# Vision tower block on one core: first embedding issued before the constants, first feed-forward group prepared inside the attention pass, third group's first score tile ahead of the value products

## The reference, cut to what matters

```python
h = _L0_tok_ref(x, W, b)                                   # patches @ W.T + b
h = concatenate([cls_tok, h], axis=1)                      # (128, 197, 256)
h = h + attn(layernorm(h))    # 16 heads of 16; q and k pass through low-rank maps and an RMS norm,
                              # causal softmax, output map per head
h = h + ffn(layernorm(h))     # 3 cycles of: coupling = 0.1 + ar*(0.7*gf + 0.3*tf - 0.5)*2
                              #              out = out + coupling * twist(out)
# tf: four-layer net per token (256-256-128-64-1); gf: three-layer net on the token mean, once
```

## Time and profile before

| what | value |
|---|---|
| median of 3 runs | 3697.5 us (3697.17 to 3704.69) |
| the profiled execution | 3697.29 us |
| its span in the trace | 3694.3 us |
| PE busy | 3538.2 us (96% of the span) |
| DVE busy | 3062.1 us (83%) |
| ACT busy | 2420.7 us (66%) |
| POOL busy | 1808.5 us (49%) |
| mean granted TensorE clock | 0.991 of full speed |

### The profile page before, as it was taken

The page is one execution under the profiler, slowest core; times in us unless marked ns, Lnnn a source line. Parts: engine busy times, 40 slices in busy tenths (PEclk is TensorE's granted clock), DMA queues, the critical chain, the costliest instruction groups (busy, mean ns, idle before and its releaser), DMA issues.

```text
span 3694.3 us, 86493 instructions
## 1 busy us (share of the span) xinstructions
PE 3538.2 (96%) x30479; PEld 2654.2 (72%) x30734; DVE 3062.1 (83%) x7295; ACT 2420.7 (66%) x5698; POOL 1808.5 (49%) x2960
## 2 busy tenths in 40 slices
PE   6999999999999999999999999996999999999998
PEld 5888888888888888888888888874555555555554
DVE  6888888888888888888888888875989989989987
ACT  3777777777777777777777777773554554554553
POOL 3666766667666776667766776663001101101000
PEclk9999999999999999999999999997999999999999
DMA  3444444444444444444444444433212222222211
GB/s 99 111 112 114 116 115 112 115 111 119 113 110 115 115 119 110 113 111 119 119 104 113 117 119 104 116 88 92 69 56 79 74 59 78 73 61 78 73 44 53
DMA packets 298315, 361.65 MB, mean 98 GB/s; under 512 B 28193, under 2 KB 264993, under 8 KB 297889
## 3 DMA queue, kind: packets, MB, share of 16 engines
q1 hardware_dynamic: 297888, 356.11, 36.7%
HBM read 131.80 MB, written 53.26 MB: 50 GB/s over the span
## 4 chain that ended last, share of the span: by engine, by line
PE 77%; DVE 9%; DMA 8%; issue 3%; SPq 1%; POOL 1%; ACT 1%; another core or an unknown queue 0%; DVEq 0%; POOLq 0%; ACTq 0%
PE ps L1357 12%; PE ps L1052 11%; PE ps L1100 7%; PE ps L1087 6%; PE ps L1366 6%; PE ps L1170 5%; PE ps L1124 5%; PE ps L1139 5%; PE ps L1189 4%; DMA mx_scratch<-mxT 4%; PE ps L1179 3%; DMA qZ<-mx_scratch 3%; PE ps L1381 2%; PE ps L1373 2%; PE ps L1147 2%
## 5 line engine op out<-in xcount | busy, mean ns | idle before, releaser
L1052 PE MATMUL ps<-xb,w_tok 128*128 128x196 f32 x3072 | 684.7, 347 | 0.3 <-DVE small L766 0.3
L862 DVE TENSOR_REDUCE mx<-ps 69x2 f32<-69x396 f32 x1024 | 520.8, 557 | 147.2 <-PE ps L1179 147.2
L1357 PE MATMUL ps<-X,cn_w 128*128 128x394 f32 x1536 | 584.5, 510 | 0.4 <-issue 0.4
L558 ACT ACTIVATE p<-ps 128x394 f32<-128x394 f32 x1024 | 454.5, 499 | 122.1 <-PE ps L1100 112.0
L1052 PEld LDWEIGHTS ps<-xb,w_tok 128*128 128x128 f32 x3072 | 490.3, 191 | 0.4 <-issue 0.4
L856 DVE TENSOR_REDUCE mx<-ps 128x4 f32<-128x512 f32 x512 | 339.0, 683 | 168.7 <-remote 168.0
L538 POOL TENSOR_SCALAR ve<-mv 128x4 f32<-128x4 f32 x64 | 19.8, 310 | 920.5 <-DVE mv L921 920.5
L1357 PEld LDWEIGHTS ps<-X,cn_w 128*128 128x128 f32 x1536 | 273.9, 190 | 250.5 <-issue 94.9
L1100 PE MATMUL ps<-qZ,kT 128*128 128x396 f32 (+1 forms) x2048 | 379.4, 319 | 48.2 <-DMA qZ<-mx_scratch 46.6
L509 POOL TENSOR_TENSOR h<-h,att 128x256 f32<-128x256 f32 (+1 forms) x256 | 187.3, 752 | 410.7 <-DVE att L851 410.7
L470 POOL TENSOR_SCALAR_AFFINE_SELECT p<-p 128x512 f32<-128x512 f32 x512 | 338.0, 660 | 78.0 <-ACT p L558 60.5
(11 more groups left out here) (140 smaller groups left out, 7932.2 us busy)
## 6 DMA issues: line engine op xcount, KB each, us to landing
qZ<-qT SPq DMA_DIRECT2D x256, 396.0 KB, 5.2
xb<-in_x SPq DMA_DIRECT2D x128, 588.0 KB, 7.2
kZ<-kT SPq DMA_DIRECT2D x512, 128.0 KB, 2.7
h_scratch<-h SPq DMA_DIRECT2D x128, 128.0 KB
hl<-h_scratch SPq DMA_DIRECT2D x64, 256.0 KB
hk<-h_scratch SPq DMA_DIRECT2D x64, 256.0 KB
out<-hk SPq DMA_DIRECT2D x64, 256.0 KB
h_scratch<-h SPq DMA_DIRECT2D x128, 69.0 KB
```

What stands on the lines that cost most here:

```text
L558: s.activation(p0[:, i, 2 * jj:2 * jj + 2, :], ps[:, (b0, b1)[jj], 0:2 * TE].rearrange("p (a b) -> p a b", b=TE)[:, :, 0:T], ACT.Exp).then ...
L862: v.tensor_reduce(mx[:T1, 1, 4 * i + c:4 * i + 4:2], ps[:T1, SBANK[3 * i + 1 + c], 0:2 * TE].rearrange("p (a b) -> p a b", b=TE), AX.X, AL ...
L1052: mm = t_.matmul(ps[:, W[ft], 0:NP], w_tok[:, k, ft * P:ft * P + P], xb[:, par, k, :], start=k == 0, stop=k == KT - 1)
L1357: mm = t_.matmul(ps[:, 2 * c + mt, 0:N2], cn_w1[:, f, mt * P:mt * P + P], X[:, c, state(cyc), f, :], start=f == 0, stop=f == FT - 1)
```

## The change

1. **Preamble.** The loads are split: `w_tok`, `tok_bT` and `clsT` on a semaphore `s_e` with the first image between them; nine small ones (`s_w`); the second image; 17 later ones (`s_w2`). The order on SP's queue is `w_tok`, image 0, `tok_bT`, `clsT`, the nine, image 1, the 17. PE embeds image 0 after `s_e`, the image and the two cleared banks; the weight products move behind this embedding into step -3. The clearing of `qkv`, `k2`, `q2`, `qZ` and `kZ` moves from DVE to POOL, behind its masks; SP's and ACT's steps wait for it. DVE's seven constants for the second pass move behind its last step.
2. **Between the passes.** `hl` of quad 0 is loaded by SP in step 126 (`n == B - 2`). DVE's `stats2` for its four pieces and `apply2` for two are put in step 129, `apply2` for the other two in step 130; POOL's `norm2` for pieces 0 and 1 stands in step 129 ahead of the masking of the exponents (`select`), for 2 and 3 behind it. `hl`, `hn2`, `st2`, `ve2`, `rstd2` move to addresses behind those of the first pass. PE waits for the last value division (`att_ready`) and then transposes quad 0. The three layers of `gnet` for quad 0 go between the layers of the first phase, in banks `GB0`.
3. **Each step.** `scores_first(m, 2)`, with its wait for the second half of `kZ`, moves ahead of both `pv`. Banks 0 and 1 change places in `SBANK` from the third group on, in `KB`, `QB`, `MB` and `CB`; the first tile of the third group so waits for two maxima instead of four.
4. **End.** For pieces 2 and 3 of the last quad, both `bases` come before both `update`.

```diff
-        SBANK = (6, 7, 0, 1, 2, 3, 0, 1, 2, 3, 0, 5)
-        MAX_OF = (4, 2, 5, 6, 7)
+        SBANK = (6, 7, 0, 1, 2, 3, 1, 0, 2, 3, 1, 5)
+        MAX_OF = (2, 4, 5, 6, 7)
-        KB, QB = (3, 4, 0, 5), (1, 2, 3, 4)
+        KB, QB = (3, 4, 1, 5), (0, 2, 3, 4)
-        MB, CB = 0, (1, 2)
+        MB, CB = 1, (0, 2)
...
+        GB0 = ((5, 6), (7, 4), (5, 6))
...
         def _(sp):
-            for dst, src in small_w:
-                sp.dma_start(dst, src).then_inc(s_w, 16)
...
+            sp.dma_start(w_tok[:], a["w_tok"]).then_inc(s_e, 16)
             load_x(0, 0)
+            sp.dma_start(tok_bT[:], a["tok_bT"]).then_inc(s_e, 16)
+            sp.dma_start(clsT[:], a["clsT"]).then_inc(s_e, 16)
+            for dst, src in small_w:
+                sp.dma_start(dst, src).then_inc(s_w, 16)
             load_x(1, 1)
-
-            sp.wait_ge(s_cv, 1)
+            for dst, src in later_w:
+                sp.dma_start(dst, src).then_inc(s_w2, 16)
+
+            sp.wait_ge(s_cv, 3)
             sp.wait_ge(s_pwc, 5)
...
             sp.wait_ge(s_cv, N_CV)
+            sp.wait_ge(s_cp, N_CP)
+            sp.wait_ge(s_kz, 1)
...
+                if n == B - 2:
+                    for p2 in range(2):
+                        sp.wait_ge(h1_stored[p2], 16 * 8 + 1)
+                    for c in range(4):
+                        load2(hl, 0, c, hl_loaded)
...
-            for c in range(4):
-                load2(hl, 0, c, hl_loaded)
             for c in range(4):
                 load2(hk, 0, c, hk_loaded)
...
+            g.memset(qkv[:], 0.0).then_inc(s_cp, 1)
+            g.memset(k2[:].bitcast(F32), 0.0).then_inc(s_cp, 1)
+            g.memset(q2[:].bitcast(F32), 0.0).then_inc(s_cp, 1)
+            pool.wait_ge(s_cp, 12)
+            g.memset(qkv[:, :, :, V, :, HD:HD + 1].rearrange("p a t h o -> p (a t) h o"), 1.0).then_inc(s_cp, 1)
+            g.memset(k2[:, :, :, 3, 0:1].bitcast(F32), 1.0).then_inc(s_cp, 1)
+            g.memset(qZ[:].bitcast(F32), 0.0).then_inc(s_cp, 1)
...
             def step(n, r):
                 if there(n - 3):
                     residual(n - 3, (r + 1) % 4)
+                if n == B + 1:
+                    norm2(0, 0)
+                    norm2(0, 1)
                 if there(n):
                     k_weighted(n, r, 0)
                 if there(n - 2):
                     for i in range(4):
                         select(n - 2, i)
+                if n == B + 1:
+                    norm2(0, 2)
+                    norm2(0, 3)
...
+            g.memset(kZ[:].bitcast(F32), 0.0).then_inc(s_kz, 1)
...
                 if there(n - 3):
                     attend(n - 3)
+                if n == B + 1:
+                    for c in range(4):
+                        stats2(0, c)
+                    apply2(0, 0, True)
+                    apply2(0, 1, True)
+                if n == B + 2:
+                    apply2(0, 2, True)
+                    apply2(0, 3, True)
...
             for c in (2, 3):
                 bases(QUADS - 1, CYCLES - 1, c)
+            for c in (2, 3):
                 update(QUADS - 1, CYCLES - 1, c)
...
         def _(dve):
             v = nc.vector
-            v.memset(w_qkv[:], 0.0).then_inc(s_cv, 1)
-            v.memset(qkv[:], 0.0).then_inc(s_cv, 1)
-            v.memset(qZ[:].bitcast(F32), 0.0).then_inc(s_cv, 1)
-            v.memset(kZ[:].bitcast(F32), 0.0).then_inc(s_cv, 1)
-            v.memset(q2[:].bitcast(F32), 0.0).then_inc(s_cv, 1)
...
             images(dve, step)
...
+            dve.wait_ge(s_w2, N_W2)
+            v.tensor_copy(cn_w4r[:], cn_w4[:, 0:1].to_broadcast([2 * F3, P])).then_inc(s_ff, 1)
...
+            dve.wait_ge(s_ff, 7)
...
+            def weight_products():
+                pe.wait_ge(s_w, N_W)
...
+                pe.wait_ge(s_cv, N_CV)
+                pe.wait_ge(s_pwc, 5)
+                pe.wait_ge(s_cp, 10)
...
                     if there(z):
+                        if z == 0 and part == 0 and ft == 0:
+                            pe.wait_ge(s_e, 48)
+                            pe.wait_ge(s_cv, 2)
...
                 embed_part(1, 2)
+                if n == -3:
+                    weight_products()
...
                 if there(x):
                     hn_transpose(x, 0)
                     hn_transpose(x, 1)
+                if there(m):
+                    pe.wait_ge(kZ_loaded[1], n * 32)
+                    scores_first(m, 2)
...
                 if there(m):
                     pe.wait_ge(kZ_loaded[1], n * 32)
-                    scores_first(m, 2)
                     scores_halves(m, 1 - r % 2, 2)
...
+            pe.wait_ge(att_ready, 2 * B)
             for c in range(4):
                 x_transpose(0, c)
-            for c in range(4):
-                pe.wait_ge(x_ready[c], 2)
-            for l in range(3):
-                for G in range(2):
-                    gnet(0, G, l)
-            for G in range(2):
-                pe.wait_ge(g_ready[G], 3)
+
+            def gnet0(start, l):
+                if start:
+                    for c in (2, 3):
+                        pe.wait_ge(x_ready[c], 2)
+                    for G in range(2):
+                        gnet(0, G, l)
...
                 layer1(i, cyc, 2 * G, 1)
                 if there_:
                     layer4(oi, ocyc, O)
+                gnet0(not there_, 0)
...
                 layer1(i, cyc, 2 * G + 1, 1)
+                gnet0(not there_, 1)
...
                 layer2(i, cyc, 2 * G)
+                gnet0(not there_, 2)
```

More of the change, by code:

```diff
@@ L528, in step @@
                     norm(n + 2, 1)
+            g.memset(kZ[:].bitcast(F32), 0.0).then_inc(s_kz, 1)
             pool.wait_ge(s_cv, N_CV)
-            pool.wait_ge(s_w, N_W)
             images(pool, step)
[L535 to L542, removed]
+            for i in range(1, QUADS):
                 for c in range(4):
@@ L649, in _ @@
             act.wait_ge(s_cv, N_CV)
[L650 removed]
+            act.wait_ge(s_cp, N_CP)
             images(act, step)
@@ L705, in _ @@
                 gelu1(i, cyc, 2 * G)
+                gnet0(start, 0)
                 if oi >= 0:
@@ L715, in _ @@
                 gelu2(i, cyc, 2 * G)
+                gnet0(start, 2)
                 if cyc == CYCLES - 1 and i + 1 < QUADS:
@@ L864, in max_halves, with stats2, apply2 @@
                                     AX.X, ALU.max, negate=True).then_inc(s_max, 1)
+            def stats2(i, c):
+                dve.wait_ge(hl_loaded[c], i * 32 + 32)
+                for k in range(4):
+                    t, n = divmod(k, 2)
+                    v.bn_stats(st2[:TS[t], c, k, :], hl[:TS[t], c, t, n, :]).then_inc(bn2_done[c // 2], 1)
+                dve.wait_ge(bn2_done[c // 2], i * 8 + 4 * (c % 2) + 4).then_inc(dve_waits, 1)
+                for k in range(4):
+                    M = TS[k // 2]
+                    v.bn_aggr(mv2[:M, c, k, :], st2[:M, c, k, :]).then_inc(mv2_ready[c // 2], 1)
+            def apply2(i, c, first):
+                dve.wait_ge(rstd2_done[c // 2], i * 2 + c % 2 + 1)
+                if not first:
+                    dve.wait_ge(x_done[c], i * 2)
+                for k in range(4):
+                    t, n = divmod(k, 2)
+                    M = TS[t]
+                    v.tensor_scalar(hn2[:M, c, k, :], hl[:M, c, t, n, :], mv2[:M, c, k, 0:1],
+                                    rstd2[:M, c, k:k + 1], ALU.subtract, ALU.mult).then_inc(hn2_ready[c], 1)
             def step(n, r):
@@ L988, in _ @@
             for c in range(4):
-                stats2(0, c)
-            for c in range(4):
-                apply2(0, c, True)
-            for c in range(4):
                 gsums(0, c)
@@ L1407, in _ @@
                 there_ = oi >= 0
+                if i == 0 and cyc == 0 and G == 1:
+                    for g in range(2):
+                        pe.wait_ge(g_ready[g], 3)
                 fresh = ocyc == CYCLES - 1 and oi + 1 < QUADS
```

132 lines of the change are left out of this document (59 added, 73 removed).

## The result

The changed kernel takes 3655.3 us (median of 4 runs, 3654.1 to 3658.8) against 3699.0 us for the kernel before on the same chip (4 runs, 3697.2 to 3704.7). The ratio is 0.9881, interval [0.9864, 0.9898].

A forecast was written before the change was run, and what follows sets the result against it. PE was taken to set the pace in the steady steps (97% busy), with room only in its gaps at the start and between the passes. 3697.3 - 9.4 + 5.0 - 15.8 + 0 - 1.3 = 3675.8, said as 3676; range 3657 to 3689.

The forecast's parts named there:

- Term 4: Each steady step: moving the third group's first tile ahead of `pv` changes nothing, 0 us, 128 times; bounds -12 and +10.
- the step pays too: Rival, steady step: the early tile brings maxima sooner, shrinking PE's 39.7 us wait; half 3656, all 3636; chance 0.11.
- Term 1: Start: the first embedding moves to about 7 us and image 2 comes earlier, -9.4 us; bounds 0 and 11.4 gained.
- Term 2: Step 126: the maxima's store queues behind quad 0's `hl` loads, delaying the rest of the pass, +5.0 us; bounds 0 and 8.
- they slip past: Rival, step 126: the maxima's store passes the `hl` stream, so no 5 us delay; 3671 us; chance 0.15.
- Terms 3 and 5: Between the passes, PE gets X sooner, -15.8 us; at the end, `bases` moves into a DVE wait, -1.3 us.
- POOL's clearing: Rival, start: at 1.56 ns a word clearing bounds the start and its gain goes; 3685 to 3689 us; chance 0.12.
- The second half of `kZ`: Rival, each step: it lands too late for the early tile; at 0.5 us a step 3740 us; chance 0.07.

The follow-up runs named there:

- e2: The changed kernel with the third group's first tile put back behind both value products, banks as changed: 3672.7 us, ratio 0.9947 to the kernel before.
- e8: The kernel before with only the new bank lists, instruction order unchanged: 3690.2 us, ratio 0.9998.
- e1: The kernel before with only the step's edit, the third group's first tile ahead of both value products and the banks changed: 3671.0 us, ratio 0.9944.
- r1: The changed kernel run again on another chip, as reference for later runs: 3649.8 us, ratio 0.9886 to the kernel before.
- e10: The changed kernel with quad 0's `hl` loads spread over steps 123 to 126 and quad 1's `hl` ahead of quad 0's `hk`: 3636.2 us, ratio 0.9849.
- e3: The changed kernel with the third group's first tile between the two value products: 3684.2 us, ratio 0.9982 to the kernel before.
- e9: The changed kernel with the second of two layer-norm transposes put between the value products, tile still early: 3695.1 us, ratio 1.0008 to the kernel before.
- e4: The changed kernel with POOL clearing only `qkv` and DVE clearing `k2`, `q2`, `qZ` and `kZ`: 3650.4 us, ratio 0.9890 to the kernel before.
- e5: The changed kernel with quad 0's `hl` loaded one piece a step in steps 123 to 126: 3646.2 us, ratio 0.9884 to the kernel before.
- e6: The changed kernel with quad 1's `hl` issued ahead of quad 0's `hk`: 3641.2 us, ratio 0.9870 to the kernel before.

## Why the prediction was wrong, step by step

**Term 4, the step: this is the step that failed.** The prediction put "0 us, 128 times", on the sentence "After `pv` PE does the same as before, at the same time". It costed each instruction by its own duration, which doesn't change with its place. What it missed is what lies between two instructions of different kinds on PE. The kinds here are products over the whole array (transposes, tiles, masks), `pv`, whose 17-column products sit side by side in four column positions, and the halves and `project`, whose 64-row products sit in two row positions. The order decides how often PE turns from one kind to another:

| order | turns from the transposes to the halves | stretch | ratio |
|---|---|---|---|
| before (and e2, e8): transposes, `pv`, tile, halves | 3 | 8.43 | 1 (e8 0.9998) |
| after (and e1, r1, e10): transposes, tile, `pv`, halves | 2 | 8.28 | e1 0.9944 |
| e3: transposes, `pv`, tile, `pv`, halves | 4 | 8.55 | 0.9982 |
| e9: transposes, tile, `pv`, transposes, `pv`, halves | 4 | 8.64 | 1.0008 |

The stretch times 128 gives the time in each pair that differs by the order alone: after to e3 0.27 x 128 = 35 us, measured by the ratios 0.9982 and 0.9886 as 35; after to e9 0.36 x 128 = 46, measured 45.3; before to e1 0.15 x 128 = 19, measured 21. So a turn is worth 0.12 to 0.15 us, and up to 0.18 where small transposes that were hidden come into the open (e9). That the cost goes with the turns is shown, by four orders, which move it in both directions, and by the starts of single products (medians from 100 to 2400 us): whatever follows `pv`, be it tile, halves or transposes, starts 0.15 us after its last product, and `pv` 0.15 us after a transpose, where in the changed kernel the tile starts 0.03 us after one (in e9, with only two transposes ahead of it, 0.17; what ends that wait isn't shown). Why a turn costs isn't shown. The weight loads that the view of the waits lists as standing don't tell it, since they are as many before as after.

The Trainium skill, *TensorEngine Tiling (Array Packing)*, "Key Properties", says that changing the tiling mode, and not just the tile, drains TensorE. The runs agree with it in that every change of kind costs time, and give the price that it doesn't name; that the array is drained is not seen in them. *TensorE: Matmul & The Clock Gate*, part 3, "The mechanism", adds that a weight load overlaps products in flight only where the row group differs. As it stands the trace doesn't agree: in the step of the changed kernel above, the four loads of the transposes run from 1205.65 to 1206.07, and their products, most of them over the same rows, start from 1205.71 on.

The prediction could have seen it: the waits of the kernel before have the halves' weight load standing three times a step with no releaser, and in its timeline the first group behind `pv` starts 0.23 us after `pv`'s last group, where groups within `pv` follow after 0.12. Its rival, *the step pays too*, named 3656 us for half of its gain and came out next to the time, by the wrong mechanism: it wanted earlier maxima and a shorter wait for them. The wait went from 39.0 to 34.4 us; r1, the same kernel, shows 29.9, and e8 29.2 without any gain. The steps as a whole are 24.3 us shorter in the trace; 0.15 x 126 = 19 of it is the stretch, and the rest is of the size that e8 shows between executions.

**Term 1, the start: -9.4, measured -8.4.** Right in size, by two errors that nearly cancel. The clearing was said to cost nothing, since it ends ahead of SP's block copies. It ends at 18.7, earlier than the forecast 21.0, but DVE's copies were held to its end, so the block copies were issued at 19.99 instead of 17.1, and the third embedding started at 29.18 instead of 26.0: 3.2 us. Against that, the 2.0 us for PE's cold start didn't appear: the gain at that row, 37.42 - 29.18 = 8.2, is kept to the first `kZ` issue (8.4). That this comes so near to 9.4 is luck in part: the first `kZ` issue is at 58.4 and 58.5 us in e1 and e8, which have the old start, and between 51.3 and 53.6 in the runs with the new one, so the gain lies between 5 and 9 us. The Trainium skill, *SBUF — State Buffer*, "Who interferes with whom" and the section on the two sides ahead of it, describes an exclusive lock between GpSimd and those DVE operations that use the shared port pair. The copies and casts here behave so, while DVE's clearings ran beside POOL's (in e4 from 3.07 to 12.42 us beside POOL's 7.35 us from 3.21 on). That page has the lock held for a whole instruction; here DVE didn't get in between seven of POOL's in a row. e4 frees the copies (0.22 us for 11.30), which shows the cause; in its trace the 2.4 us won at the third embedding are 0.3 at the first `kZ` issue, and the low clock behind the longer wait is a part of that loss.

**Term 2, step 126: +5.0, measured +6.8.** The mechanism was right: the maxima are read back after 6.75 us where 6 was said. The stream's issue takes 8.79 us of SP (5.89 in the earlier trace rows) and the store's own issue 1.30 for 0.31. The rival that they slip past falls. In e1 and e8, with the old loading, this way takes 48.5 and 49.6 us, in the other runs with the new one 54.0 to 54.7, so the price is 4 to 7 us. e5 takes 4.7 us of it away.

**Terms 3 and 5, between the passes and the end: -15.8 and -1.3, measured -17.2 together.** Their sum was 17.1. `layer1` starts 27.4 us earlier after that store (26 forecast), and quad 1's first `hl` piece comes 12.2 us earlier (11.4 forecast; 2532.51 - 2512.56 = 19.95 against 2570.61 - 2538.44 = 32.17). `layer1` of the second cycle starts 18.7 us sooner after the last `h1` store (17 forecast), and with the clock granted at 0.50 from 2544 to 2549 us the products from there to the next eight of `layer1` take 3.0 us longer than before (7.62 for 4.61; 1.5 was taken). That PE is then held by DVE behind `hl`, as said, is shown by e6: with quad 1's `hl` first the wait goes from 7.7 to 0.4 us. Its ratio, 0.9870 against 0.9881 and 0.9886 of the changed kernel, is 4 to 6 us, with intervals that touch; with e5's edit (e10) it is 13.6 us, and beyond doubt.

**The other rivals.** POOL's clearing didn't bound the start by its length; its rate was 0.84 ns a word (7.35 us for 8704), the lower bound. The second half of `kZ` isn't late: PE's wait for `kZ` is 2.1 us in all.

With 19 to 20 us for term 4 in place of 0 the sum would have been 3656 to 3657.

## What to carry to other kernels

When PE bounds a loop, cost the order of its instructions as well as the instructions: list which products use the whole array, which row positions and which column positions, and count the turns between them in one round. Group products of one kind, and put a moved product beside its own kind; read start to start at every turn in the timeline, for the turn that was saved here stood in no list of waits. And when clearing moves to POOL, see what DVE copies or casts at that time: its length then counts even where nobody waits for the cleared buffers.

## What the runs showed of the hardware

- A turn of PE between whole-array and row- or column-positioned products costs 0.12 to 0.15 us here; what follows `pv` starts 0.23 us after the start of its last group, its own next group after 0.12.
- Behind the bf16 mask product the first weight load of `pv` or of the halves stands 0.23 us, in every step and order; the time saved by one turn fewer is not part of it.
- Two copies of 128x2 words and two casts of 128x128 on DVE, ready at 7.4 to 7.7 us, ended at 18.8 to 18.9, when POOL's chain of clearings ended (3.20 to 18.73); without the chain a cast took 0.22 us.
- A 16-row store behind eight 256 KB and 138 KB loads on one queue was read back after 6.75 us; behind two of them, issued 5.8 us earlier, after 1.38.
- Where the clock falls at the start differs between executions of one kernel: granted 0.83 and 1.00 from 20 to 44 and 44 to 56 us in one, 0.93 and 0.72 in the other.
